# One decoder layer on one core: the second expert matmul of the late tiles as three products of rounded parts, one tile later, and the last tile added by one-hot matmuls

## The chip, the cores and the metric

The kernel runs on one core of a Trainium2 chip. The time is that of one execution on the device, in microseconds (us); the numbers shown are medians over runs of the same program on the same inputs.

## The reference

One decoder layer: self-attention, cross-attention to 1500 context rows, and a mixture of experts, each followed by a residual sum and a layer norm. The change lies in the third part, for 16 x 56 = 896 tokens of width 256, 8 experts of hidden width 1024 and two experts per token:

```python
def _L0_ffn_ref(inputs, gate_w, gate_b, w1, b1, w2, b2):
    gate_probs = softmax(x @ gate_w + gate_b, axis=-1)
    weights, selected = jax.lax.top_k(gate_probs, 2)
    weights = weights / jnp.sum(weights, axis=-1, keepdims=True)
    comb = jnp.zeros((n, E)).at[arange(n)[:, None], selected].set(weights)
    h = jax.nn.gelu(jnp.einsum('nd,edf->enf', x, w1) + b1[:, None, :])
    expert_out = jnp.einsum('enf,efd->end', h, w2) + b2[:, None, :]
    return jnp.einsum('ne,end->nd', comb, expert_out)
x = _layernorm(x + _L0_attn_ref(x, ...)); x = _layernorm(x + _L0_xattn_ref(x, ctx, ...))
x = _layernorm(x + _L0_ffn_ref(x, ...))
```

## The kernel before

The attention parts take the first 740 us of the span and are not touched. Each token's row, with its two gate values, is scattered by GpSimd into `xs` in DRAM, sorted by expert in groups of 128 rows. The residual rows (the input of the experts) go to `sums` in DRAM.

The expert stage works through `GT` = 21 tiles `g` of 128 sorted rows, each of one expert. A table `e_tab` names the expert of a tile; its first `EARLY` = 5 entries are known early, the rest after the last tokens are routed (`at["late tiles known"]`). All of `w2` (8 experts, 8 blocks of 128 x 256 each) lies in SBUF in `w2_sb`; `w1` of the tile's expert (1 MB) is loaded for each tile into one of two buffers. The steps of a tile are:

- SyncE: `load_xg(g)` loads the 128 rows when `gate(g-2)` has read the buffer (`row_read`); `load_w1(g)` loads the weights when the first matmuls of tile g-2 are done (`m1_done`). All of this stands in one queue, in order.
- TensorE: `tx(g)` transposes the rows (2 matmuls), `m1(g)` in two halves of 8 matmuls each with 128 columns makes the hidden values, `m2(g)` in 8 fp32 matmuls of 256 columns the output. `m2(g)` waits for the gelu of its tile.
- ScalarE: `gelu_half(g, i)`, four activations of 128 x 128 for each half, into `hT`.
- VectorE: `xgT_step(g)` copies the transposed rows out of PSUM, `gate(g)` makes the gate value from six small operations, `y_step(g)` scales `b2` (L918), and forms gate x output + gate x b2 (L924) in `y_sb`.
- GpSimd: `add(g)` adds the rows of `y_sb` to `sums` in DRAM by an indirect DMA (L1245); each waits until the one before has landed.

A sub-block of `w2_sb` is picked by a register that is read from `e_tab` (`value_load`), on each engine that needs the expert. TensorE's order is `tx(g)`, `m2(g-1)`, `m1(g)` for each late tile: `m2(g-1)` is the work beside which gelu and the copies run.

The end: when all 21 additions have landed (`added`), SyncE loads `sums` in four parts of two token tiles (`sum_in[q]`, L1116) into `acc`. VectorE makes statistics of each part (L967, L970, L972), GpSimd the power -1/2 (L1274), and ScalarE (parts 0 and 2) or VectorE (parts 1 and 3, `normalise`, L960) the normalised rows, which SyncE stores.

PSUM has eight banks. Banks 1 to 4 (`H_BANK` + 0 to 3) hold the hidden values of two tiles, banks 6 and 5 (`Y_BANKS`) the outputs.

For keys and values of the attention part the kernel already uses products of rounded parts: a tensor is written once in the type float32r (`ctx_hi`, `wkv_hi`), the rest beside it (`ctx_lo`, `wkv_lo`), and three products (hi hi, hi lo, lo hi, the list `SPLIT`) are summed in PSUM (`unit`, L1514 and L1521).

## Time and profile before

| | us |
|---|---|
| median of 3 runs | 913.03 (911.96 to 915.29) |
| the profiled execution, its own time | 917.23 |
| its span, first to last instruction | 915.4 |
| TensorE busy in the span | 830.5 (91%) |
| VectorE, ScalarE, GpSimd busy | 599.3, 465.5, 267.4 |

Instruction names give the output and the inputs without the digits at a name's end or before an underscore (`w2_sb` is shown as `w_sb`). One fp32 matmul stands in the trace as two records, one float32r matmul as one. A matmul's shown duration is longer than the distance to the next one, since they are pipelined; the pace is read from the start times. "PEclk" is the granted clock of TensorE: 1.00 is 2.4 GHz and 0.50 is 1.2 GHz.

### The profile page before, as it was taken

How to read it: one execution, taken by the hardware profiler on the slowest of the kernel's cores; microseconds unless marked ns; L12 is line 12 of the kernel's file. 1: busy time of each engine (PE TensorE's matmuls, PEld its weight loads, DVE VectorE, ACT ScalarE, POOL GpSimd, SP SyncE). 2: the span in 40 equal slices, each digit the busy share in tenths (PEclk: the TensorE clock that was granted, in tenths of full speed). 3: DMA queues.
4: the chain of work that ended last, by engine and by line, in shares of the span. 5: the costliest groups of instructions: out<-in, count | busy, mean ns of one | idle time of the engine just before them, and what ended most of it. 6: DMA issues, size and time to landing. Idle time of an engine off the chain costs nothing.

```text
span 915.4 us, 29917 instructions
## 1 busy us (share of the span) xinstructions
PE 830.5 (91%) x12210; PEld 669.4 (73%) x12210; DVE 599.3 (65%) x1308; ACT 465.5 (51%) x1050; POOL 267.4 (29%) x341
## 2 busy tenths in 40 slices
PE   5789999999999989999999999999997889999992
PEld 3567876777777767777777777777775589999991
DVE  5867677777787758777787777777864734222222
ACT  2355565655565546555665655556654443332232
POOL 5142224122612251244215232612240103222222
PEclk9899999999999999999999999999999699999997
DMA  6355545454454545545455455544474646766643
GB/s 214 108 168 155 155 121 159 131 148 131 141 162 133 143 130 154 149 148 162 136 144 175 131 155 143 166 125 144 142 251 163 260 170 188 182 184 190 189 124 98
DMA packets 91092, 143.56 MB, mean 157 GB/s; under 512 B 11378, under 2 KB 79794, under 8 KB 87120
## 3 DMA queue, kind: packets, MB, share of 16 engines
q1 hardware_dynamic: 86592, 132.59, 48.4%
q0 software_dynamic: 4368, 9.08, 4.4%
q8 instruction: 99, 1.62, 0.8%
q14 instruction: 33, 0.27, 0.1%
HBM read 101.60 MB, written 39.94 MB: 155 GB/s over the span
## 4 chain that ended last, share of the span: by engine, by line
PE 60%; DMA 15%; ACT 8%; DVE 7%; SPq 5%; issue 4%; POOL 0%; DVEq 0%; POOLq 0%; ACTq 0%
PE ps L1521 11%; DMA k_dram<-k_two 11%; PE ps L1514 9%; PE ps L1831 8%; PE ps L1852 8%; PE ps L1595 6%; PE ps L1573 5%; PE ps L1537 4%; SPq L1006 3%; ACT k_two L1297 3%; DMA k_st<-k_dram 3%; ACT pT L1324 2%; DVE negmax L484 2%; DVE k_two L478 2%; PE ps L1638 2%
## 5 line engine op out<-in xcount | busy, mean ns | idle before, releaser
L484 DVE TENSOR_REDUCE negmax<-ps 112x1 f32<-112x1500 f32 x121 | 207.3, 1713 | 42.0 <-PE ps L1537 41.0
L1324 ACT ACTIVATE pT<-ps 125x448 f32<-125x448 f32 x384 | 196.1, 547 | 22.4 <-PE ps L1573 18.4
L1155 POOL TENSOR_TENSOR ctx_lo<-ctx_raw,ctx_hi 128x250 fp32r<-128x250 f32 x188 | 130.5, 726 | 234.7 <-DVE ctx_hi L469 234.7
L1573 PE MATMUL ps<-qbd,k_st 98*128 98x112 f16 x1536 | 130.1, 216 | 17.2 <-ACT qbd L1280 8.1
L1573 PEld LDWEIGHTS ps<-qbd,k_st 98*128 98x128 f16 x1536 | 87.4, 99 | 76.2 <-ACT qbd L1280 23.1
L478 DVE SCALAR_TENSOR_TENSOR k_two<-ps,bk_sb,k_two 128x500 f16<-128x500 f32 x96 | 70.7, 736 | 88.3 <-ACT k_two L1297 88.2
L1297 ACT ACTIVATE k_two<-ps,bk_sb 128x500 f16<-128x500 f32 x96 | 65.0, 677 | 95.7 <-PE ps L1514 77.3
L1280 ACT COPY v_sb<-ps 125x512 f32<-125x512 f32 x96 | 56.3, 587 | 105.6 <-PE ps L1521 105.6
L1595 PE MATMUL ps<-pT,v_sb 125*17 125x56 f32 x6144 | 92.8, 217 | 8.3 <-issue 8.3
L1537 PE MATMUL ps<-k_st,qbd 96*112 96x500 f16 x363 | 96.9, 374 | 2.9 <-issue 2.4
L1595 PEld LDWEIGHTS ps<-pT,v_sb 125*17 125x17 f32 x6144 | 81.1, 100 | 24.5 <-issue 18.1
L1452 ACT ACTIVATE hT<-ps,b_col 128x128 f32<-128x128 f32 x168 | 48.0, 368 | 99.9 <-PE ps L1831 99.9
L1521 PE MATMUL ps<-wkv_hi,ctx_hi 128*125 128x256 f32 x384 | 88.2, 311 | 6.2 <-DVE k_two L478 4.1
L1831 PE MATMUL ps<-xgT,w_sb 128*128 128x128 f32 x672 | 80.6, 279 | 0.0
L1831 PEld LDWEIGHTS ps<-xgT,w_sb 128*128 128x128 f32 x672 | 79.9, 195 | 1.0
L1521 PE MATMUL ps<-wkv_hi,ctx_lo 128*125 128x256 f32 x384 | 77.7, 284 | 2.7 <-issue 2.7
L1521 PE MATMUL ps<-wkv_lo,ctx_hi 128*125 128x256 f32 x384 | 77.5, 283 | 0.0
L1852 PE MATMUL ps<-w_sb,hT 128*128 x336 | 76.2, 380 | 0.6 <-issue 0.6
L1521 PEld LDWEIGHTS ps<-wkv_hi,ctx_hi 128*125 128x125 f32 x384 | 60.7, 189 | 21.7 <-issue 18.6
L1514 PE MATMUL ps<-ctx_hi,wkv_hi 128*128 128x500 f32 x192 | 68.4, 438 | 7.6 <-ACT v_sb L1280 3.4
L1245 POOL DMA_INDIRECT sums<-y_sb,g_token x21 | 32.9, 1567 | 137.4 <-DVE y_sb L924 134.2
L1852 PEld LDWEIGHTS ps<-w_sb,hT 128*128 128x128 f32 x336 | 62.1, 190 | 8.7 <-issue 1.1
(238 smaller groups left out, 1220.5 us busy)
## 6 DMA issues: line engine op xcount, KB each, us to landing
k_st<-k_dram SPq DMA_DIRECT2D x288, 125.0 KB, 2.6
w_sb<-w SPq DMA_DIRECT2D x25, 1024.0 KB, 5.7
ctx_raw<-ctx_T SPq DMA_DIRECT2D x48, 500.0 KB, 4.3
k_dram<-k_two SPq DMA_DIRECT2D x96, 250.0 KB, 3.7
xs<-zeros SPq DMA_DIRECT2D x28, 260.0 KB
w_sb<-w POOLq DMA_DIRECT2D x4, 1024.0 KB, 9.5
xg<-xs SPq DMA_DIRECT2D x21, 130.0 KB, 4.7
a_x<-x_tok SPq DMA_DIRECT2D x8, 128.0 KB, 2.4
```

Source lines behind the costliest of these rows:

```text
L478: V.scalar_tensor_tensor(k_two[:, i, 1], ps[:, BANK_KV, 0:MC], bk_sb[:, g:g + 1], k_two[:, i, 0], ALU.add, ALU.subtract).then_inc(unit_out, 1)
L484: V.tensor_reduce(negmax[0:QW], ps[0:QW, BANK_S:BANK_S + CHUNKS, 0:MC], AX.XY, ALU.max, negate=True).then_inc(max_done, 1)
L1155: last = nc.gpsimd.tensor_tensor(ctx_lo[:, k, c2, a], ctx_raw[:, k, c2, a], ctx_hi[:, k, c2, a].bitcast(F32), ALU.subtract)
L1297: nc.scalar.activation(k_two[:, i, 0], ps[:, BANK_KV, 0:MC], ACT.Identity, bias=bk_sb[:, g:g + 1]).then_inc(k_hi_done, 1)
L1324: nc.scalar.activation(pT[0:MT, (PAIRS * b + p) % 3, TPC * g:TPC * g + TPC], ps[0:MT, BANK_T + n % 2, 0:TPC * QW].rearrange("p (t n) -> p ...
L1514: last = mm(ps[:, BANK_KV, 0:MC], ws[w][:, k, P * g:P * g + P], cs[x][:, place, k, :], start=(i == 0 and k == 0), stop=(i == 2 and k == CH ...
L1521: last = mm(ps[0:MT, BANK_KV, D * m:D * m + D], cs[x][:, place, k, a:a + MT], ws[w][:, k, D:2 * D], start=(i == 0 and k == 0), stop=(i == ...
L1537: last = mm(ps[0:QW, BANK_S + c, 0:MC], qbd[0:KS, j, p].rearrange("p h s -> p (h s)"), k_st[0:KS, j, p, MC * c:MC * c + MC], start=True, s ...
L1573: last = mm(ps[:, BANK_T + n % 2, QW * i:QW * i + QW], k_st[:, j, p, a:a + P], qbd[:, j, p].rearrange("p h s -> p (h s)"), start=True, sto ...
L1595: last = mm(ps[32 * i:32 * i + VW, BANK_O, QW * (p % 4) + S * hp:QW * (p % 4) + S * hp + S], v_sb[0:MT, j, m, 2 * p + hp], pT[0:MT, (PAIRS ...
L1831: last = mm(ps[:, H_BANK + 2 * par + i, P * q:P * q + P], w1_sb[:, par, c, P * f:P * f + P], xgT[:, par, c], start=(c == 0), stop=(c == CH ...
L1852: last = mm(ps[:, Y_BANKS[g % 2], 0:D], hT[:, g % 2, f], w2_sb[:, bass.ds(e, 1), f].rearrange("p a n -> p (a n)"), start=(f == 0), stop=(f ...
```

## The change

For tiles 5 to 20, ScalarE writes `w2_hi` (2048 columns, the tile's expert copied to float32r) and `h_hi` (1024 columns, the gelu's output copied to float32r); VectorE writes the differences `w2_lo` and `h_lo`. `m2_split(g)` makes 24 float32r matmuls of 256 columns instead of 8 fp32 matmuls, and TensorE's order becomes first half of `m1(g)`, `tx(g+1)`, second half of `m1(g)`, `m2_split(g-1)`. `w2_hi(g)` waits until `m2_split(g-2)` is done (two buffers).

The last tile is no longer added in DRAM. SyncE waits for 20 additions, TensorE brings each loaded part of the sums into PSUM by a product with the identity (`carried(q)`, fp32, 512 columns) and adds, for each of 8 token tiles, a one-hot matrix times `y_sb` (fp32, 256 columns). The one-hot matrices are made by VectorE from `token_row`. Statistics and normalisation read the sums from PSUM.

```diff
@@ -235,10 +235,16 @@
         xg = sb("xg", [P, 2, XW])
         xgT = sb("xgT", [P, 2, CH, P])
         y_sb = sb("y_sb", [P, 2, D])
-        sb("to_values", [P, 6392])
+        w2_hi = sb("w2_hi", [P, 2, FT, D], F32R)
+        h_hi = sb("h_hi", [P, 2, FT, P], F32R)
+        sb("to_values", [P, 248])
         b2_all = sb("b2_all", [P, E, D])
         hT = sb("hT", [P, 2, FT, P])
         g_b2 = sb("g_b2", [P, 4, D])
+        token_row = sb("token_row", [P, P])
+        token_hot = sb("token_hot", [P, TILES, P])
+        w2_lo = sb("w2_lo", [P, 2, FT, D], F32R)
+        h_lo = sb("h_lo", [P, 2, FT, P], F32R)
         kv_in = sem("kv_in")
         dec_in = sem("dec_in")
@@ -899,6 +917,8 @@
                 one = slice(q, q + 1)
                 if g == EARLY:
                     dve.wait_ge(p_dve, at["late tiles known"])
+                if g > EARLY:
+                    dve.wait_ge(added, 16 * (g - 3))
                 V.scalar_tensor_tensor(g_num[:, one], row[:, D + 2:D + 3], e_sum[:, g:g + 1], row[:, D + 1:D + 2],
                                        ALU.is_equal, ALU.max).then_inc(gate_step, 1)
                 V.tensor_scalar(g_den[:, one], row[:, D + 1:D + 2], 1.0, None, ALU.add).then_inc(gate_step, 1)
@@ -947,24 +967,52 @@
             gate(3)
             late_table()
             y_step(2)
-            for g in range(3, GT):
+            xgT_step(4)
+            gate(4)
+            y_step(3)
+            xgT_step(EARLY)
+            gate(EARLY)
+            y_step(EARLY - 1)
+
+            def w2_lo_step(g):
+                e = dve.value_load(e_tab[0:1, g:g + 1], min_val=0, max_val=E - 1)
+                dve.wait_ge(w2_hi_done, g - EARLY + 1)
+                V.tensor_tensor(w2_lo[:, g % 2], w2_sb[:, bass.ds(e, 1)].rearrange("p a f n -> p (a f) n"),
+                                w2_hi[:, g % 2].bitcast(F32), ALU.subtract).then_inc(w2_lo_done, 1)
+
+            def h_lo_step(g):
+                dve.wait_ge(h_hi_done, g - EARLY + 1)
+                V.tensor_tensor(h_lo[:, g % 2], hT[:, g % 2], h_hi[:, g % 2].bitcast(F32),
+                                ALU.subtract).then_inc(h_lo_done, 1)
+
+            for g in range(EARLY, GT):
                 if g + 1 < GT:
                     xgT_step(g + 1)
+                w2_lo_step(g)
+                if g + 1 < GT:
                     gate(g + 1)
-                y_step(g)
+                h_lo_step(g)
+                if g > EARLY:
+                    y_step(g - 1)
+                if g == GT - 1:
+                    dve.wait_ge(row_kept, 1)
+                    for t in range(TILES):
+                        V.tensor_scalar(token_hot[:, t], token_row[:], float(P * t + 1), xg[:, (GT - 1) % 2, D:D + 1],
+                                        ALU.add, ALU.is_equal).then_inc(hot_made, 1)
+            y_step(GT - 1)
             def normalise(q):
                 dve.wait_ge(f_rstd, q + 1)
                 for t in (2 * q, 2 * q + 1):
-                    V.tensor_scalar(o_all[:, t], acc[:, t], mv8[:, t, 0:1], sm[:, 5, t:t + 1],
+                    V.tensor_scalar(o_all[:, t], last_sum(t), mv8[:, t, 0:1], sm[:, 5, t:t + 1],
                                     ALU.subtract, ALU.mult).then_inc(f_out[q], 1)
             for q in range(TILES // 2):
                 two = slice(2 * q, 2 * q + 2)
-                dve.wait_ge(sum_in[q], 16)
+                dve.wait_ge(hot_done, 2 * q + 2)
                 for t in (2 * q, 2 * q + 1):
-                    V.bn_stats(st8[:, t], acc[:, t]).then_inc(f_stat, 1)
+                    V.bn_stats(st8[:, t], last_sum(t)).then_inc(f_stat, 1)
                 for t in (2 * q, 2 * q + 1):
                     dve.wait_ge(f_stat, 2 * q + t + 1)
                     V.bn_aggr(mv8[:, t], st8[:, t]).then_inc(f_stat, 1)
@@ -1111,7 +1159,7 @@
                 load_xg(g)
                 load_w1(g)
-            sp.wait_ge(added, 16 * GT)
+            sp.wait_ge(added, 16 * (GT - 1))
             for q in range(TILES // 2):
                 sp.dma_start(acc[:, 2 * q:2 * q + 2], sums_tiles[2 * q:2 * q + 2].rearrange("t p n -> p t n")).then_inc(sum_in[q], 16)
             out_rows = out.rearrange("(t j) p n -> j p t n", j=2)
@@ -1265,7 +1313,7 @@
             add(1)
             scatter(TILES - 1)
             pool.wait_ge(sums_last, 16)
-            for g in range(2, GT):
+            for g in range(2, GT - 1):
                 add(g)
             for q in range(TILES // 2):
@@ -1460,15 +1508,32 @@
             gelu_half(1, 0)
             gelu_half(1, 1)
             b_step(4, TILES - 1)
+            def w2_hi_step(g):
+                act.wait_ge(p_dve, at["late tiles known"])
+                e = act.value_load(e_tab[0:1, g:g + 1], min_val=0, max_val=E - 1)
+                act.wait_ge(m2_done, g - 1)
+                copy(w2_hi[:, g % 2], w2_sb[:, bass.ds(e, 1)].rearrange("p a f n -> p (a f) n")).then_inc(w2_hi_done, 1)
+
+            def h_hi_step(g):
+                act.wait_ge(gelu_done, 2 * g + 2)
+                copy(h_hi[:, g % 2], hT[:, g % 2]).then_inc(h_hi_done, 1)
+
             for g in range(2, GT):
+                if g >= EARLY:
+                    w2_hi_step(g)
+                if g == EARLY:
+                    act.wait_ge(row_made, 1)
+                    copy(token_row[:], ps[:, BANK_O, 0:P]).then_inc(row_kept, 1)
                 gelu_half(g, 0)
                 gelu_half(g, 1)
+                if g >= EARLY:
+                    h_hi_step(g)
             for q in (0, 2):
                 act.wait_ge(f_mean, q // 2 + 1)
                 act.wait_ge(f_rstd, q + 1)
                 for t in (2 * q, 2 * q + 1):
-                    nc.scalar.activation(o_all[:, t], acc[:, t], ACT.Identity, bias=sm[:, 6, t:t + 1]).then_inc(f_centre, 1)
+                    nc.scalar.activation(o_all[:, t], last_sum(t), ACT.Identity, bias=sm[:, 6, t:t + 1]).then_inc(f_centre, 1)
                 for t in (2 * q, 2 * q + 1):
                     act.wait_ge(f_centre, t + 1 - q)
                     nc.scalar.activation(o_all[:, t], o_all[:, t], ACT.Copy, scale=sm[:, 5, t:t + 1]).then_inc(f_out[q], 1)
@@ -1853,6 +1918,17 @@
                               w2_sb[:, bass.ds(e, 1), f].rearrange("p a n -> p (a n)"), start=(f == 0), stop=(f == FT - 1))
                 last.then_inc(m2_done, 1)
+            def m2_split(g):
+                par = g % 2
+                pe.wait_ge(y_ready, g - 1)
+                pe.wait_ge(w2_lo_done, g - EARLY + 1)
+                pe.wait_ge(h_lo_done, g - EARLY + 1)
+                for f in range(FT):
+                    for i, (x, w) in enumerate(SPLIT):
+                        last = mm(ps[:, Y_BANKS[par], 0:D], (h_hi, h_lo)[x][:, par, f], (w2_hi, w2_lo)[w][:, par, f],
+                                  start=(f == 0 and i == 0), stop=(f == FT - 1 and i == 2))
+                last.then_inc(m2_done, 1)
+
             last_tile = TILES - 1
             pe.wait_ge(p_dve, at["early tiles known"])
             tx(0)
@@ -1882,11 +1958,32 @@
             m2(3)
             m1(4)
             pe.wait_ge(p_dve, at["late tiles known"])
+            tx(EARLY)
+            m2(EARLY - 1)
+            pe.wait_ge(y_ready, EARLY - 1)
+            mm(ps[:, BANK_O, 0:P], ones16[:], before16[:], start=True, stop=True).then_inc(row_made, 1)
             for g in range(EARLY, GT):
-                tx(g)
-                m2(g - 1)
-                m1(g)
-            m2(GT - 1)
+                m1_half(g, 0)
+                if g + 1 < GT:
+                    tx(g + 1)
+                m1_half(g, 1)
+                if g > EARLY:
+                    m2_split(g - 1)
+            m2_split(GT - 1)
+
+            def carried(q):
+                pe.wait_ge(sum_in[q], 16)
+                mm(ps[:, H_BANK + q].rearrange("p (t n) -> p t n", t=2), id32[:], acc[:, 2 * q:2 * q + 2],
+                   start=True, stop=False)
+
+            carried(0)
+            carried(1)
+            pe.wait_ge(y_ready, GT)
+            for t in range(TILES):
+                if t % 2 == 0 and t > 2:
+                    carried(t // 2)
+                pe.wait_ge(hot_made, t + 1)
+                mm(last_sum(t), token_hot[:, t], y_sb[:, (GT - 1) % 2], start=False, stop=(t % 2 == 1)).then_inc(hot_done, 1)
 # ---- launch: one core; the arrays only change their layout ----
```

TensorE's queue at a late tile, before (two matmul rows of the eight; "ISA" sets the address from the register). This is the place after `m1(4)`:

```order
L1831 MATMUL ps<-xgT,w_sb 128x128 x16
L1482 MATMUL ps<-id,xg 128x128 x2
L1810 TENSOR_LOAD e_tab
L1810 ISA x2
L1852 ISA
L1852 MATMUL ps<-w_sb,hT 128x256
L1852 ISA
L1852 MATMUL ps<-w_sb,hT 128x256
```

The same queue of the changed kernel, from the end of `m2(4)` on (L1896 is `m1_half`, L1547 the transposes, L1928 `m2_split`, of whose 24 rows three stand here):

```order
L1964 MATMUL ps<-before,ones 128x128
L1896 MATMUL ps<-xgT,w_sb 128x128 x8
L1547 MATMUL ps<-id,xg 128x128 x2
L1896 MATMUL ps<-xgT,w_sb 128x128 x16
L1547 MATMUL ps<-id,xg 128x128 x2
L1896 MATMUL ps<-xgT,w_sb 128x128 x8
L1928 MATMUL ps<-w_hi,h_hi 128x256
L1928 MATMUL ps<-w_lo,h_hi 128x256
L1928 MATMUL ps<-w_hi,h_lo 128x256
```

The second matmuls of tile 5 now stand behind the first ones of tile 6; before they stood ahead of them.

VectorE's queue of the changed kernel through one late tile (L912 `xgT_step`, L978 and L980 `w2_lo_step`, L922 to L930 `gate`, L985 `h_lo_step`, L934 to L944 `y_step` of the tile before):

```order
L912 COPY xgT<-ps 128x256 [waits tx_done]
L978 TENSOR_LOAD e_tab
L978 ISA x2
L980 ISA [waits w2_hi_done]
L980 TENSOR_TENSOR w_lo<-w_sb,w_hi 128x2048
L922 SCALAR_TENSOR_TENSOR g_num<-xg,e_sum 128x1 [waits added]
...
L930 TENSOR_TENSOR g_gate<-g_num,g_rec 128x1 [waits gate_step]
L985 TENSOR_TENSOR h_lo<-hT,h_hi 128x1024 [waits h_hi_done]
L934 TENSOR_LOAD e_tab
...
L938 TENSOR_SCALAR g_b<-b_all,g_gate 128x256
L944 SCALAR_TENSOR_TENSOR y_sb<-ps,g_gate,g_b 128x256 [waits added,m2_done,gate_done]
```

Before, the queue held `xgT_step`, `gate` and `y_step` alone; `w2_lo` and `h_lo` and a second register load have come in.

TensorE's last rows of the changed kernel (L1976 is `carried`, L1986 the one-hot products), which have no counterpart before:

```order
L1976 MATMUL ps<-rows_all,id 128x512 x2
L1986 MATMUL ps<-y_sb,token_hot 128x256 x4
L1976 MATMUL ps<-rows_all,id 128x512
L1986 MATMUL ps<-y_sb,token_hot 128x256 x2
L1976 MATMUL ps<-rows_all,id 128x512
L1986 MATMUL ps<-y_sb,token_hot 128x256 x2
```

Two identity products stand ahead of the first one-hot products, so the statistics of part 0 come after four products.

## Rows read from the trace of the kernel before

**Rows 1.** The page: busy time, and the granted clock in 40 slices

```profile
PE 830.5 (91%) x12210; PEld 669.4 (73%) x12210; DVE 599.3 (65%) x1308; ACT 465.5 (51%) x1050; POOL 267.4 (29%) x341
PEclk9899999999999999999999999999999699999997
```

**Rows 2.** The chain that ended last, 700 to 916 us: start, us, what

```profile
886.71 0.22 PE ps L1482 x2
886.92 3.46 PE ps L1852 x16
890.38 3.57 PE ps L1831 x32
893.95 3.52 PE ps L1852 x16
...
897.55 0.49 DVE y_sb L924
...
898.79 3.72 DMA sums<-y_sb,g_token
```

**Rows 3.** Stretches: us; busy PE, PEld, DVE, ACT, POOL; PEclk; DMA share; GB/s

```profile
780.00:890.00 110.00, 110.00 (x757) 103.49 (x756) 29.82 (x136) 34.31 (x120) 23.39 (x15) 1.00 0.65 178
```

**Rows 4.** Timeline of TensorE, 300 to 312 us: start, us, what

```profile
304.66 0.40 PE L1521 MATMUL ps<-wkv_lo,ctx_hi 128*125 128x256 f32 x2
...
305.60 0.40 PE L1521 MATMUL ps<-wkv_hi,ctx_lo 128*125 128x256 f32 x2
```

**Rows 5.** Lines L439 and L1280: duration ns min/median/max, first and last start

```profile
L439 DVE TENSOR_TENSOR wkv_lo<-pT,wkv_hi x1: 1224/1224/1224, 6.1 to 6.1; 128x1024 fp32r<-128x1024 f32 x1
...
L1280 ACT COPY v_sb<-ps x96: 586/587/592, 15.1 to 698.1; 125x512 f32<-125x512 f32 x96
L1280 ACT COPY a_oT<-ps x8: 372/372/373, 33.9 to 627.0; 128x256 f32<-128x256 f32 x8
L1280 ACT COPY rows_all<-b_x x8: 407/431/433, 193.0 to 758.7; 128x256 f32<-128x256 f32 x8
```

**Rows 6.** Timeline of one late tile, 845 to 870 us

```profile
850.61 1.14 ACT L1452 ACTIVATE hT<-ps,b_col 128x128 f32<-128x128 f32 x4 [0.66 <-PE ps L1831]
850.66 0.42 DVE L894 COPY xgT<-ps 128x256 f32<-128x256 f32 x1 [3.25 <-PE ps L1482]
851.00 0.21 DVE L902 SCALAR_TENSOR_TENSOR g_num<-xg,e_sum 128x1 f32<-128x1 f32 x1
...
851.70 0.16 DVE L910 TENSOR_TENSOR g_gate<-g_num,g_rec 128x1 f32<-128x1 f32 x1
```

**Rows 7.** Timeline of the end, 890 to 916 us

```profile
890.47 0.48 DVE L924 SCALAR_TENSOR_TENSOR y_sb<-ps,g_gate,g_b 128x256 f32<-128x256 f32 x1 [1.36 <-PE ps L1852]
891.25 0.35 DVE L918 TENSOR_SCALAR g_b<-b_all,g_gate 128x256 f32 x1 [0.29 <-issue]
...
902.52 1.95 SPq L1116 DMA_DIRECT2D rows_all<-sums  x4
905.25 0.75 DVE L967 BATCH_NORM_STATS2 st<-rows_all 128x6 f32<-128x256 f32 x2 [7.21 <-DMA rows_all<-sums]
...
909.41 0.75 DVE L967 BATCH_NORM_STATS2 st<-rows_all 128x6 f32<-128x256 f32 x2
```

**Rows 8.** Stretches of the end and of two earlier places, columns as in Rows 3

```profile
897.50:898.50 1.00, 0.00 (x0) 0.00 (x0) 0.48 (x1) 0.00 (x0) 0.00 (x0) 1.00 0.00 0
...
901.50:902.00 0.50, 0.00 (x0) 0.00 (x0) 0.00 (x0) 0.00 (x0) 0.00 (x0) 0.81 0.87 131
902.00:904.00 2.00, 0.00 (x0) 0.00 (x0) 0.00 (x0) 0.00 (x0) 0.00 (x0) 0.50 0.13 36
...
22.00:27.80 5.80, 5.80 (x18) 2.96 (x19) 5.33 (x11) 0.63 (x1) 0.34 (x1) 0.50 0.52 122
...
741.50:744.70 3.20, 3.20 (x17) 3.20 (x16) 1.10 (x3) 0.00 (x0) 0.00 (x0) 0.50 0.00 0
```

**Rows 9.** DMA queue, issues from 770 to 900 us: KB each, median us to landing

```profile
w_sb<-w SPq DMA_DIRECT2D x16, 1024.0 KB, 5.7
```

More of the change, by code:

```diff
@@ L346, in decoder_layer @@
         sums_last = sem("sums_last")
+        row_made = sem("row_made")
+        w2_hi_done = sem("w2_hi_done")
+        w2_lo_done = sem("w2_lo_done")
+        h_hi_done = sem("h_hi_done")
+        h_lo_done = sem("h_lo_done")
+        row_kept = sem("row_kept")
+        hot_made = sem("hot_made")
+        hot_done = sem("hot_done")
         tail_set = sem("tail_set")
@@ L398, in home, with last_sum @@
             return BANK_S if t == 0 and k in (2, 4, 6) else BANK_A
+        def last_sum(t):
+            return ps[:, H_BANK + t // 2, D * (t % 2):D * (t % 2) + D]
         def key_place(par, c, g):
```

## The prediction

> **What bounds the kernel now.** I read the page first: TensorE is busy for 91% of the span, and its granted clock is at the full level in nearly every slice but the last [rows 1]. The attention part is untouched, so only the stretch after 778 us matters. There the stretch view says it plainly: from 780 to 890 us TensorE is busy for 110.00 of 110.00 us at clock 1.00, VectorE for 29.82 and ScalarE for 34.31 [rows 3]. The chain that ended last holds nothing but TensorE in that stretch, one tile after the other: transposes 0.22, second matmuls 3.46, first matmuls 3.57, so 7.25 us a tile [rows 2]. TensorE's time per tile is what a change can win. After the last tile the bound changes: output scaled (897.55 to 898.04), addition landed at 902.51, loads of the sums issued from 902.52, first statistics at 905.25, statistics of part 3 at 909.41, end of the span at 915.4 [rows 2, 7]. I call the end of the last tile's first matmuls T, before 893.95: the tail behind T is 21.45 us long.
>
> **The tiles: TensorE.** The second matmuls of tiles 5 to 20 become 24 float32r products of 256 columns. The kernel has this form already, in the value units of the attention part: with weights of 125 columns instead of 128, two matmuls start at 304.66 and the fifth pair at 305.60, so four pairs take 0.94 us and one matmul 0.1175 us [rows 4]. An fp32 one takes 3.46 / 8 = 0.4325 us [rows 2], so three products are 0.35 against 0.43, and a tile's 24 are 2.82 us against 3.46. Bounds: 2.82 if the pace holds, 3.46 if the change of form gains nothing; I take 2.82, since shape and form are the same but for three columns. Before T, fifteen second matmuls of late tiles stood (5 to 19); now fourteen do (5 to 18), since they come one tile later. So T comes 15 x 3.46 - 14 x 2.82 = 51.9 - 39.5 = **12.4 us earlier**, if nobody makes TensorE wait. The one bf16 product for `token_row` and its copy are below 0.5 us and are left out. A tile now takes 0.22 + 3.57 + 2.82 = 6.61 us.
>
> **The tiles: the engines beside it.** ScalarE gets a copy of 2048 and one of 1024 columns. Copies of 512 and 256 columns take 0.587 and 0.372 us [rows 5], 0.84 ns a column, which gives 1.88 and 1.02 us; in proportion to the larger copy, the upper bound, it is 2.35 and 1.17. With the two gelu halves of 1.14 each [rows 6] that is 5.2 to 5.8 us a tile, under 6.61. `w2_hi(g)` may start when `m2_split(g-2)` ends, which is just the start of `m1(g)`; it ends some 1.9 us later, about when the first half of `m1(g)` (1.79 us) is done, so gelu is hardly late.
>
> VectorE is the tighter one. Per tile: copy 0.42 [rows 6]; register load, of which 0.36 shows (from the start of the operation ahead to the one behind the load 0.78 us pass in the row pair 890.47 and 891.25 [rows 7], less 0.42 of work); `w2_lo` at most twice the 1.224 us that the same subtraction takes at 1024 columns, 2.45 [rows 5]; gate 851.00 to 851.86, 0.86 [rows 6]; `h_lo` 1.22; `y_step` 0.35 + 0.48 [rows 7]; four waits at some 0.05. Sum 6.34 against 6.61. Cover: counted from the start of `m1(g)`, `h_lo(g)` ends at about 7.5 us, and `m2_split(g)` wants it at 6.61 + 3.79 = 10.4, so 2.9 us are in hand. If VectorE needs x us a tile, TensorE loses 14 (x - 6.61) - 2.9 us in all: nothing up to x = 6.8.
>
> Weights: `w1(g+2)` is asked for when `m1(g)` ends, at 3.8 us after its start, and lands 5.7 later [rows 9], at 9.5 to 10; it is wanted at 13.2. The rows of `xg` are asked for after each `gate` and have two tiles. `add(g)` takes 4.5 us from y to landing [rows 2], against 6.61 a tile, so the new wait in `gate` (addition g-3) is long over. All this costs nothing as long as it lies beside 6.61 us of TensorE.
>
> **The tail.** From the new T: the second half of gelu ends at T + 1.35, `h_hi` at + 2.4, `h_lo` at + 3.65, `y_step(19)` (it stands behind `h_lo(20)`) at + 4.6. `m2_split(19)` ended at + 2.8, so TensorE waits 0.9 us, then makes `m2_split(20)` until + 6.5; `y_sb` of tile 20 is ready near + 7.5, with the eight one-hot matrices made beside it. Addition 19 lands 4.5 after + 4.6, the first sums 2.7 after that: **T + 11.8**. Before, the first sums were there at T + 11.3: the spared addition is paid back by the last output's place one tile further back.
>
> Then comes what is new: TensorE must make 4 identity products of 512 columns (2 x 0.4325 = 0.865 each) and 8 one-hot products (0.4325 each), 6.92 us at full clock [rows 2]. The clock is not full there. TensorE stopped at 897.5, and the granted clock fell to 0.50 near 901.8, 4.3 us later [rows 8]; now it stands still from + 6.5 to + 11.8. How soon it returns: in two stretches in which TensorE was busy without a pause, it was at 0.50 for 3.2 us (from 741.5) and for 5.8 us (from 22.0) [rows 8]. I take 5 us. In these 5 us half the work is done, 2.5, and the rest takes 4.4: the last one-hot product is done 9.4 us after the first sums. Statistics of part 3 cannot start before `normalise(1)` is over, at about + 9.9, and from them to the end it is 6.0 us as before (909.41 to 915.4) [rows 7]. End: T + 11.8 + 9.9 + 6.0 = T + 27.7, against T + 21.45. The tail costs **6.2 us more**.
>
> By the Trainium skill (TensorE: Matmul & The Clock Gate, "What's actually happening") the array sits at 1.2 GHz by default and goes back to it when idle; the clock column of this trace agrees, with 0.50 after the stop.
>
> **Sum.** -12.4 + 6.2 = -6.2 us. The profiled execution has a span of 915.4 in a time of 917.23, 4.2 above the median; the differences are taken to be the same for both. 913.03 - 6.2 = 906.8, so **907**.
>
> **Rivals.**
> - **The clock stays low through all twelve products** (a 0.50 stretch of 5.8 us is in the trace, and the twelve have pauses only if sums land late). 13.8 us instead of 9.4 and no wait for `normalise`: + 4.0, 910.8. Chance 0.1.
> - **The clock does not fall, or comes back at once.** The products take 6.9 us, and part 3 starts at + 7.2: - 2.7, 904.2. For it: the pause is only 5.3 us, little over the 4.3 after which it fell. Chance 0.15.
> - **Addition 19 is held up by the one-hot matrices.** They stand directly behind `y_step(19)` on VectorE, when GpSimd prepares this addition, which everything behind waits for. Eight operations of about 0.2 us (the 256-column one is 0.35 [rows 7]) are 1.6 us: 908.4. In the trace of before no VectorE work lies beside an addition's preparation at the end, so it shows neither. Chance 0.08. The Trainium skill (SBUF — State Buffer, "SBUF: two separate sides") says that GpSimd cannot write its descriptors while VectorE runs an operation in a two-port mode; no row here shows it.
> - **VectorE becomes the bound (slower).** By the formula above the gain is gone at x = 7.26 us a tile and the time is 0.5% above before (917.6) at x = 7.6, that is 1.2 us over my sum; for instance if the register loads or the 2048 columns cost half as much again. Against it: every part but `w2_lo`'s length has a row. 913 to 918, chance 0.07.
> - **The float32r products don't keep their pace.** At 0.144 us each a tile's second matmuls stay at 3.46; only the shift by one tile is left: - 3.5 + 6.2, 915.7. For it: in the units the weights have 125 columns, here 128. Chance 0.05.
> - Something unpriced (rows or weights late, a wait at the first split tile): 909 to 914, chance 0.05.
>
> My forecast itself has 0.5 and its own range is 905 to 909.
>
> **How the numbers follow.** A measurement of this kernel tells about 0.5% (4.6 us) from no change, so faster is below 908.5. From the forecast's 0.5 some 0.43 lie below, from the high-clock case all 0.15, from the held addition 0.04: 0.62. Slower (above 917.6) is what is left of the VectorE and pace cases with some for the unknown, 0.08. Same 0.30. The range reaches down to the high-clock case and up past the low-clock one: 903.5 to 912.5.
>
> **What the profile after would show.** Right: 6.6 us between `m2_split` groups with TensorE busy throughout, 24 matmuls at 0.118 us; VectorE at 5.5 to 6.4 us a tile with its wait on transposes still there; T near 881.5; first sums near T + 11.8; clock at 0.50 when the first identity product starts. Wrong: TensorE waiting for `h_lo` in every tile (VectorE), 3.4 us for a tile's 24 products (pace), clock 1.00 in the tail, or an addition landing later than 4.5 us after y.

## Result

The changed kernel takes 905.09 us (median of 20 runs, 900.23 to 914.34), the kernel before 914.44 us (20 runs, 906.66 to 925.74). The ratio, taken over the executions outside the slower state that a few of them fell in, is 0.9925, 95% interval 0.9901 to 0.9948: 6.9 us less, between 4.8 and 9.1. The two medians are 9.4 us apart, just outside that interval; single executions of one kernel scatter by 14 to 19 us, so I go by the ratio. Forecast was 6.2 us less.

The profiled execution of the changed kernel has a span of 905.0 us, against 915.4 before. Of these 10.4 us only a part belongs to the change: the first matmuls of tile 0 start at 736.91 instead of 741.51, after a part of the program in which no instruction differs. Over the 14 profiles of this study that start lies between 729.4 and 743.6 us with no relation to the edit, while the stage behind it was 128.1 and 127.7 us in two traces of the changed kernel. Of the kernel before there is one trace, but from M to T, defined below, the run with the one-hot end alone, which has the same instructions there, agrees with it within 0.1 us (112.4 and 112.3). So I compare kernels by the stage from the end of tile 4's second matmuls (M) to the end of the span: 133.8 us before (781.63 to 915.4), 128.1 after (776.90 to 905.0). **The change is worth 5.7 us in the traces.**

The chain of the changed kernel, start, us, what. The first rows are tiles 4, 5 and 18 (L1917 second matmuls in fp32, L1928 the split ones, L1896 the first ones), the others the end:

```profile
773.44 3.46 PE ps L1917 x16
...
784.63 3.07 PE ps L1928 x24
787.70 1.78 PE ps L1896 x16
789.48 0.22 PE ps L1547 x2
789.70 1.79 PE ps L1896 x16
791.49 2.83 PE ps L1928 x24
...
870.93 2.83 PE ps L1928 x24
873.76 3.58 PE ps L1896 x32
...
882.58 3.92 DMA sums<-y_sb,g_token
...
886.51 2.73 DMA rows_all<-sums
...
889.29 3.78 PE ps L1976 x4
893.07 2.25 PE ps L1986 x8
```

The second matmuls take 2.83 us instead of 3.46 [rows 2], the tile 6.62 instead of 7.25. The first matmuls of tile 20 end at T = 877.34, so M to T is 100.4 us; before it was 112.3. The tail behind T is 27.7 us long instead of 21.45.

The stretches, columns as in Rows 3: TensorE has no pause up to T, VectorE is busy for 82 of 100 us, and the clock falls in the pause before the sums land and comes back at 894.

```profile
776.90:877.30 100.40, 100.36 (x881) 100.20 (x881) 81.86 (x165) 78.95 (x155) 31.82 (x15) 1.00 0.64 190
...
886.00:887.00 1.00, 0.00 (x0) 0.00 (x0) 0.00 (x0) 0.00 (x0) 0.00 (x0) 1.00 0.03 3
887.00:888.00 1.00, 0.00 (x0) 0.00 (x0) 0.00 (x0) 0.00 (x0) 0.00 (x0) 0.58 0.20 59
...
893.00:894.00 1.00, 1.00 (x4) 0.82 (x3) 0.00 (x0) 0.00 (x0) 0.00 (x0) 0.50 0.00 0
894.00:897.00 3.00, 3.00 (x13) 2.26 (x13) 2.27 (x11) 0.41 (x2) 0.81 (x2) 1.00 0.00 0
```

One thing got worse that the span does not show. GpSimd's additions by their source line, first of the kernel before, then of the changed one. The first row has shortest, median and longest preparation in ns and the time of the first and the last; the second row the time to landing, which is counted from the start of the preparation and so contains it:

```profile
L1245 POOL DMA_INDIRECT sums<-y_sb,g_token x21: 1549/1561/1612, 752.6 to 898.8; - x21
...
DMA to landing us min/median/max: 3.6/3.8/4.2
```

```profile
L1293 POOL DMA_INDIRECT sums<-y_sb,g_token x20: 1549/2087/3229, 748.0 to 882.6; - x20
...
DMA to landing us min/median/max: 3.7/5.2/7.1
```

Preparing one takes 2.09 us in the median instead of 1.56, and preparation and landing together 5.2 instead of 3.8. From tile 6 to tile 19 every addition starts 0.78 us after the landing of the one ahead; before the change none of the late ones did, there were 3.3 us or more between them. The additions of tiles 6 to 19 start at 798.85 to 882.58, one in 6.44 us, where a tile takes 6.62: the delay that tiles 5 and 6 leave (7.1 us each to landing) is only just made up at the end. Addition 19 starts 0.78 us after its output and 0.78 us after the landing of addition 18 (both at 881.80), so two paths set the start of the sums at once. Several of the experiments below ran into this.

### The profile page after: what moved, and what is told of

Its sections match the earlier page's. It is cut to its first block, busy times and chain, and to the rows that moved or that the text cites. A ratio compares the mean times of both kernels' runs of the same rounds, so it can differ in the third digit from the quotient of the medians.

```text
span 905.0 us, 30247 instructions
## 1 busy us (share of the span) xinstructions
PE 828.6 (92%) x12363; PEld 671.4 (74%) x12363; DVE 656.6 (73%) x1348; ACT 511.9 (57%) x1083; POOL 276.5 (31%) x340
## 3 DMA queue, kind: packets, MB, share of 16 engines
q8 instruction: 99, 1.62, 0.8%
## 4 chain that ended last, share of the span: by engine, by line
PE 61%; DMA 13%; DVE 9%; ACT 8%; SPq 4%; issue 4%; DVEq 0%; POOL 0%; POOLq 0%; ACTq 0%
PE ps L1586 11%; PE ps L1579 10%; DMA k_dram<-k_two 9%; PE ps L1896 9%; PE ps L1660 7%; PE ps L1638 5%; PE ps L1928 4%; PE ps L1602 4%; ACT k_two L1345 3%; SPq L1054 3%; DMA k_st<-k_dram 3%; ACT pT L1372 2%; DVE negmax L502 2%; PE ps L1917 2%; DVE k_two L496 2%
## 5 line engine op out<-in xcount | busy, mean ns | idle before, releaser
L1203 POOL TENSOR_TENSOR ctx_lo<-ctx_raw,ctx_hi 128x250 fp32r<-128x250 f32 x188 | 130.5, 726 | 230.9 <-DVE ctx_hi L487 230.9
L1896 PE MATMUL ps<-xgT,w_sb 128*128 128x128 f32 x672 | 83.0, 279 | 0.0
L1896 PEld LDWEIGHTS ps<-xgT,w_sb 128*128 128x128 f32 x672 | 79.8, 195 | 0.3
L1293 POOL DMA_INDIRECT sums<-y_sb,g_token x20 | 42.2, 2111 | 118.1 <-DVE y_sb L944 62.0
L1232 POOL TENSOR_TENSOR qbd<-q_st,pmask 96x448 f16<-96x448 f16 x32 | 29.2, 932 | 129.4 <-DVE q_st L604 129.4
L1328 ACT COPY qbd<-ps 2x112 f16<-2x112 f16 x128 | 31.4, 245 | 61.0 <-PE ps L1624 58.9
```

The source lines that it names most:

```text
L1203: last = nc.gpsimd.tensor_tensor(ctx_lo[:, k, c2, a], ctx_raw[:, k, c2, a], ctx_hi[:, k, c2, a].bitcast(F32), ALU.subtract)
L1328: return nc.scalar.copy(dst, src)
L1896: last = mm(ps[:, H_BANK + 2 * par + i, P * q:P * q + P], w1_sb[:, par, c, P * f:P * f + P], xgT[:, par, c], start=(c == 0), stop=(c == CH ...
```

## Experiments

All stages, from M to the end of the span; T is the end of tile 20's first matmuls. Runs without a ratio were run once. Each ratio is to the kernel before as run in the same set; the sets were run on different chips.

| run | M | span | stage | ratio to before |
|---|---|---|---|---|
| before | 781.63 | 915.4 | 133.8 | 1 |
| the change | 776.90 | 905.0 | 128.1 | 0.9925 (0.9901 to 0.9948) |
| the change again | 783.51 | 911.2 | 127.7 | 0.9947 (0.9907 to 0.9987) |
| split products alone | 781.06 | 907.6 | 126.5 | 0.9933 (0.9891 to 0.9976) |
| one-hot end alone | 778.10 | 908.6 | 130.5 | 0.9952 (0.9921 to 0.9982) |
| tile 19 early | 779.04 | 907.5 | 128.5 | 0.9914 (0.9879 to 0.9949) |
| TensorE kept busy in the pause | 774.09 | 899.8 | 125.7 | 0.9926 (0.9888 to 0.9963) |
| two products of three | 772.48 | 887.5 | 115.0 | |
| 128 columns of w2_lo | 769.37 | 897.5 | 128.1 | |
| tile 19 early, tile 20 in fp32 | 774.39 | 901.4 | 127.0 | 0.9920 (0.9878 to 0.9961) |
| the same, TensorE kept busy | 776.11 | 900.5 | 124.4 | 0.9916 (0.9886 to 0.9945) |
| w2_lo twice | 778.12 | 923.1 | 145.0 | |
| tile 19 early, little w2_lo and w1 | 779.12 | 905.1 | 126.0 | |
| split alone, little w2_lo and w1 | 775.51 | 902.3 | 126.8 | |

The intervals of the ratios are 4 to 8 us wide and overlap throughout; differences of 1 to 4 us between these kernels are shown by the stages, one trace each, and not by the clocked runs.

**The change again.** The same file.

> The changed kernel as it is, beside the three others on one chip. All theories: 0.9925 of before (0.990 to 0.995), stage after the second matmuls of tile 4 near 128.1 us; the part ahead of that stage should differ from before by chance alone.

Stage 127.7 against 128.1 us: two traces of one kernel lie 0.4 us apart. The start of the stage moved by 6.7 us between them. The clocked ratio is 0.9947 and its interval holds the first one's 0.9925.

The chain that ended last takes another way here. It runs through all 15 additions from tile 5 on without a break, 797.58 to 892.98, three quarters of the stage; its last rows are:

```profile
883.34 5.20 DMA sums<-y_sb,g_token
...
889.32 3.65 DMA sums<-y_sb,g_token
...
892.99 2.71 DMA rows_all<-sums
```

Addition 18 landed at 888.54, 0.13 us after output 19 was there (888.41). So in the changed kernel the row of additions is as much the bound of the last sums as TensorE is, and in the first trace the two only met.

**Each half of the change alone.** First the split products with the end as before:

```diff
-            sp.wait_ge(added, 16 * (GT - 1))
+            sp.wait_ge(added, 16 * GT)
-            for g in range(2, GT - 1):
+            for g in range(2, GT):
                 add(g)
-                dve.wait_ge(hot_done, 2 * q + 2)
+                dve.wait_ge(sum_in[q], 16)
```

(and `last_sum(t)` is `acc[:, t]`; `token_row`, `token_hot`, `carried` and the one-hot products are gone.)

> The products of rounded parts as in the change, the last tile added in DRAM as before. Theory (what the one-hot end is worth here is negative): with the split order the sums can be loaded only 11.9 us after the last first matmuls (T) and 12 products follow at half clock; without them, tile 20's output is ready at T + 7.2, lands at T + 11.7, the first sums are there at T + 14.4, and from there 10.15 us as before: T + 24.6 instead of the changed kernel's T + 27.7. So 3.1 us less than the changed kernel, stage after the second matmuls of tile 4: 125.0 us instead of 128.1. Rival (the one-hot end saves the 4.5 us of an addition): 3 us or more above the changed kernel, stage 131 or more.

126.5 us: better than the change by 1.5 (by 1.2 than its repeat), not by 3.1. Its chain shows why:

```profile
880.81 5.10 DMA sums<-y_sb,g_token
...
886.68 3.54 DMA sums<-y_sb,g_token
...
891.00 3.77 DMA sums<-y_sb,g_token
...
894.79 2.84 DMA rows_all<-sums
```

Addition 20 starts at 891.00, after the landing of addition 19 at 890.22, while its output was ready at 888.84. I had let it start from its own output. The one-hot end costs 1.2 to 1.5 us in this order of work, by one trace of each, where its rival had it gain 3.

Then the one-hot end alone, on the kernel before (fp32 second matmuls and their order kept):

```diff
-            for g in range(2, GT):
+            for g in range(2, GT - 1):
                 add(g)
+            carried(0)
+            carried(1)
+            pe.wait_ge(y_ready, GT)
+            for t in range(TILES):
+                ...
+                mm(last_sum(t), token_hot[:, t], y_sb[:, (GT - 1) % 2], ...)
```

(`token_row`, `token_hot`, `last_sum` and the waits are as in the change.)

> The one-hot end alone, second matmuls in fp32 and in the order of before. Theory (the end is good where the last output but one is early and TensorE has no pause): addition 19 lands at T + 1.5, first sums at T + 4.2, TensorE comes from the last second matmuls at T + 3.5 without a fall of the clock, 6.9 us of products at full clock, end at T + 17.5 instead of T + 21.5: 4.0 us less than before, 909 to 911 where before is 914. Rival (the one-hot end costs its products whatever the order): at least 3 us more than before.

130.5 us, 3.2 less than before; expected 4.0. Here addition 19 runs beside the first matmuls of tile 20, and the first identity products need 0.99 us for each of the two at full clock:

```profile
888.29 3.88 DMA sums<-y_sb,g_token
...
892.19 2.99 DMA rows_all<-sums
...
895.22 1.98 PE ps L1914 x4
897.21 1.73 PE ps L1924 x8
```

So the halves are worth 7.2 and 3.2 us alone, 10.4 in sum, and 5.7 together. The traces say where the missing 4.7 us are. M to T is the same with and without the one-hot end (100.4 and 100.3 us split, 112.4 and 112.3 in fp32). From T to the first sums the one-hot end alone has 4.65 us and the change 11.9, 7.25 more; without the one-hot end it is 11.3 before and 16.25 with split products, 5.0 more. That is 2.3 us: output 19, for which the sums wait with the one-hot end, comes 4.5 us after T and not 3.0 before it, while output 20, which counts without it, moves by less. From the first sums to the end of the span the one-hot end alone takes 13.5 us, at clock 1.00 all through its products, and the change 15.7, with a pause of TensorE and a fallen clock; without the one-hot end this part is 10.2 and 10.0. That is the other 2.4, and the next run takes it away.

**The clock in the pause.**

```diff
             m2_split(GT - 1)
+            for _ in range(11):
+                mm(ps[:, BANK_S, 0:D], id32[:], w2_sb[:, 0, 0], start=True, stop=True)
```

> The changed kernel with 11 more fp32 matmuls of 256 columns on TensorE in the pause between the last split tile and the first sums; their result is not used. Theory (the clock's fall in that pause has a price): granted clock 1.00 when the first identity product starts, the twelve products take 6.9 instead of 9.4 us, of which the statistics' own pace leaves 1.5 to 2.5 us: 1.5 to 2.5 us less than the changed kernel. Rival (loads and statistics set the pace of the end): less than 0.5 us.

The granted clock is 1.00 from 880 to 892 us, and the first two identity products take 1.99 us instead of 3.78:

```profile
883.60 2.79 DMA rows_all<-sums
...
886.43 1.99 PE ps L1978 x4
888.41 1.73 PE ps L1988 x8
```

Stage 125.7 us, 2.4 less (2.0 less than the repeat). The sums land 112.3 us after M in both kernels, so all of it is behind that landing, where only the clock of the products differs. That the pause costs a clock level and that the level has this price is shown.

**Where VectorE stands.** Two products of the three:

```diff
-                    for i, (x, w) in enumerate(SPLIT):
+                    for i, (x, w) in enumerate(SPLIT[:2]):
```

> The third product (lo of the hidden values times hi of the weights) is left out in tiles 5 to 20; VectorE and ScalarE do all they did, so the output loses some precision. TensorE then needs 0.22 + 3.57 + 1.88 = 5.67 us a tile. Theory (VectorE is next, at about 6.1 to 6.2 us a tile): the tile period falls from 6.62 to 6.1 to 6.2, not to 5.67, and TensorE waits for h_lo or the transposed rows in every tile. Rival (there is room on VectorE): 5.67 to 5.8 us a tile, 14 us less in all.

The stage is 115.0 us, 13.1 less. M to T is 87.0 us instead of 100.4, 13.4 less, which is 14 x 0.96: the tile takes 5.66 us and VectorE keeps up. My theory of it as the next bound at 6.1 is refuted. Behind T nothing is won, though two more tiles are shorter there: addition 19 starts 1.55 us after its output, held by the row of additions, and the sums land 12.9 us after T instead of 11.9. VectorE's timeline through one such tile, one `y_step` (L944) to the next:

```profile
835.36 0.48 DVE L944 SCALAR_TENSOR_TENSOR y_sb<-ps,g_gate,g_b 128x256 f32<-128x256 f32 x1
835.76 0.41 DVE L912 COPY xgT<-ps 128x256 f32<-128x256 f32 x1
836.12 2.29 DVE L980 TENSOR_TENSOR w_lo<-w_sb,w_hi 128x2048 fp32r<-128x2048 f32 x1
...
839.49 1.23 DVE L985 TENSOR_TENSOR h_lo<-hT,h_hi 128x1024 fp32r<-128x1024 f32 x1 [0.31 <-ACT h_hi L1328]
840.63 0.35 DVE L938 TENSOR_SCALAR g_b<-b_all,g_gate 128x256 f32 x1
841.02 0.48 DVE L944 SCALAR_TENSOR_TENSOR y_sb<-ps,g_gate,g_b 128x256 f32<-128x256 f32 x1
```

An operation starts some 0.06 to 0.09 us before the shown end of the one ahead (835.36 + 0.48 is 835.84, the next starts at 835.76), and the register load that I had put at 0.36 us is hidden: `w2_lo` starts at 836.12, before the copy's end. In the changed kernel, where VectorE first waits 0.40 us for the transposes, the load still shows as 0.33 us without work between the copy and `w2_lo`; it vanishes when VectorE has work queued.

Then `w2_lo` twice in each tile:

```diff
                 dve.wait_ge(w2_hi_done, g - EARLY + 1)
+                V.tensor_tensor(w2_lo[:, g % 2], w2_sb[...], w2_hi[:, g % 2].bitcast(F32), ALU.subtract).then_inc(twice, 1)
+                dve.wait_ge(twice, g - EARLY + 1)
                 V.tensor_tensor(w2_lo[:, g % 2], ...
```

> The changed kernel with w2_lo computed twice in each tile, 2.3 us more of VectorE. With two products only, VectorE kept up with 5.67 us a tile, so its own need is 5.3 to 5.6 us and now 7.6 to 7.9. Theory (the formula of the prediction: nothing until the need is over 6.6 us a tile, then 14 times the excess less 2.9 us in hand): 11 to 15 us more than the changed kernel, stage 139 to 143. Rival (the 2.9 us in hand aren't there, or more waits come in): over 146.

```profile
793.11 1.22 DVE L989 TENSOR_TENSOR h_lo<-hT,h_hi 128x1024 fp32r<-128x1024 f32 x1
...
840.91 2.29 DVE L981 TENSOR_TENSOR w_lo<-w_sb,w_hi 128x2048 fp32r<-128x2048 f32 x1
843.24 2.29 DVE L984 TENSOR_TENSOR w_lo<-w_sb,w_hi 128x2048 fp32r<-128x2048 f32 x1
...
891.72 1.22 DVE L989 TENSOR_TENSOR h_lo<-hT,h_hi 128x1024 fp32r<-128x1024 f32 x1
```

Thirteen tiles in 98.61 us are 7.585 us each. The extra operation and its wait are 2.33, and VectorE's operations follow each other there with no gap of 0.05 us or more, so its own need in the changed kernel is 5.26 us a tile, against my 6.34. The stage is 145.0 us, 16.9 more: above the 139 to 143 of the theory and below the rival's 146. 14 x (7.585 - 6.61) is 13.7, and T comes 13.6 us later against M (114.0 instead of 100.4), so the 2.9 us in hand were not there. The rest (3.3) is behind T, where the doubled `w2_lo` also stands ahead of the last `h_lo`; how it divides I did not separate.

**The output of tile 19 early.**

```diff
+                if g == GT - 1:
+                    m2_split(g - 1)
                 m1_half(g, 1)
-                if g > EARLY:
+                if EARLY < g < GT - 1:
                     m2_split(g - 1)
```

(and on VectorE `y_step(GT - 2)` ahead of `h_lo_step(GT - 1)`.)

> The changed kernel with the second matmuls of tile 19 between the two halves of tile 20's first ones, and its output scaled ahead of h_lo(20). Theory (the end hangs on the output of tile 19): with s the start of tile 20's first matmuls, output 19 is ready at s + 5.1 instead of s + 8.1, first sums at s + 12.5, TensorE busy to s + 12.9 with a short pause, 12 products at full or nearly full clock: 4 to 5 us less than the changed kernel. Rival (the end hangs on TensorE's clock or on tile 20's chain through gelu, h_hi and h_lo, which gets 2.8 us later): no gain or up to 2 us more.

128.5 us: no gain, though output 19 was ready at 881.14, 2.8 us earlier against M than in the change (102.1 instead of 104.9). The chain does not hold TensorE here but additions:

```profile
872.81 5.28 DMA sums<-y_sb,g_token
...
878.87 5.24 DMA sums<-y_sb,g_token
...
884.88 4.75 DMA sums<-y_sb,g_token
...
889.65 2.73 DMA rows_all<-sums
```

Addition 19 starts at 884.88, 3.75 us after its output, because addition 18 landed at 884.10, and the first sums are there 113.3 us after M, 1.0 later than in the change. The rival had the result (no gain), but neither theory had named this cause. Two runs ask what slows the additions. First little of `w2_lo` (from tile 7 on only 128 of its 2048 columns are written, and VectorE waits there for the second matmuls of tile g-2):

> From tile 7 on VectorE writes only 128 of the 2048 columns of w2_lo, the rest keeps what tiles 5 and 6 left, so the output is not exact. TensorE does the same work. Theory (additions are slowed because GpSimd prepares them while VectorE subtracts with two inputs from SBUF): the preparations beside tiles 8 to 19 fall from 2.1 us in the median to 1.56, the landing from 5.2 to 3.8 us as before, and no addition waits for the one ahead. Rival (the denser weight loads slow them): landing stays at 5 us. Neither changes the time of the kernel by more than 1 us.

```profile
L1298 POOL DMA_INDIRECT sums<-y_sb,g_token x20: 1549/1560/1655, 740.5 to 875.0; - x20
...
DMA to landing us min/median/max: 3.7/5.8/6.8
```

The preparation falls back to 1.56 us, as the theory says: it is `w2_lo` beside it that makes it long. Preparation and landing together do not get shorter: 5.8 us, as the rival says, though 0.5 us of preparation are spared. So two things slow an addition, and they don't add up: what is spared in the preparation is spent waiting behind it. The second was tried on the kernel with tile 19 early, with little `w2_lo` and, from tile 7 on, 128 of 1024 columns of the `w1` load:

```diff
-                sp.dma_start(w1_sb[:, g % 2], w1[bass.ds(e, 1)]...)
+                n = F if g < EARLY + 2 else P
+                sp.dma_start(w1_sb[:, g % 2, :, 0:n], w1[bass.ds(e, 1), :, :, 0:n]...)
```

> Tile 19 early, and from tile 7 on only 128 of 2048 columns of w2_lo and 128 of 1024 columns of the first weights (w1) loaded, so the output is not exact; TensorE's work is the same. Theory (the chain of additions is the bound of that run: they are slowed by w2_lo in their preparation and by the w1 loads in their landing, so that addition 19 starts 3 us late): preparation 1.56 and landing 3.7 to 4.0 us, addition 19 starts 0.7 us after its output, the products start when TensorE comes from tile 20: stage 124.5 to 125.5 instead of 128.5. Rival (something else holds the end): 127.5 or more, and if landing stays over 5 us the w1 loads are not what slows it.

```profile
L1301 POOL DMA_INDIRECT sums<-y_sb,g_token x20: 1549/1561/1627, 750.2 to 882.9; - x20
...
DMA to landing us min/median/max: 3.7/3.9/4.2
```

Landing is 3.9 us, where little `w2_lo` alone left it at 5.8: it is the `w1` transfer beside it, 1 MB in each tile, which in the changed kernel is under way when the addition's rows move, and before the change had mostly landed by then. With little `w2_lo` alone, for instance, the load asked for at 843.70 landed 5.2 us later, at 848.9, and the addition begun at 844.02 landed at 849.9, just behind it. It is a matter of when and not of how much: with `w2_lo` twice the loads are full too, but their rows have moved before the addition's, and from the end of its preparation an addition takes 2.2 us to land as before the change (5.5 less 3.24). What a small `w1` load does with a full `w2_lo` was not run.

The stage is 126.0 us, 2.5 less than with full loads and 0.5 to 1.5 more than expected. Addition 19 starts 1.7 us after its output and not 0.7: outputs 18 and 19 are 3.55 us apart here, and even an unslowed addition with the 0.78 us to the next takes 4.5. The chain now goes through tile 20 instead: TensorE waits for its gelu, `h_hi` and `h_lo`, the clock falls in that pause, and the 24 products take 5.46 us instead of 2.83:

```profile
884.83 1.24 DVE h_lo L990
...
886.20 5.46 PE ps L1936 x24
```

The same reliefs on the split products alone:

> The products of rounded parts without the one-hot end, with the same two reliefs as in the run with tile 19 early (128 columns of w2_lo and of w1 from tile 7 on; output not exact). Theory: addition 20 starts 0.7 us after its output instead of after the landing of addition 19: 1.4 us less than with full loads, stage 125.1 instead of 126.5. Rival: unchanged at 126.5.

126.8 us, no gain, a miss: even at 3.75 us an addition, 20 waits for 19 (they start at 881.05 and 885.58 in its chain), since outputs 19 and 20 are 3.0 us apart. What holds that kernel is that two additions must follow each other behind output 19, and not how slow the ones ahead of them are.

**Tile 20 in fp32.** The kernel with tile 19 early, and the last second matmuls as before:

```diff
-            m2_split(GT - 1)
+            m2(GT - 1)
```

(and no `w2_hi`, `w2_lo`, `h_hi`, `h_lo` for that tile.)

> The run with tile 19 early, and tile 20's second matmuls in fp32 as before, without its hi and lo parts. Theory: the chain gelu, h_hi, h_lo behind tile 20 (3.7 us, in which TensorE stands) is spared for 0.63 us more of matmuls; the twelve products start when the sums land, 1 to 3 us earlier than with tile 19 early alone, at full clock: 5 to 7 us less than the changed kernel. Rival (the sums' landing is the bound whatever TensorE does): the same as with tile 19 early within 0.5 us.

127.0 us, 1.5 less than with tile 19 early alone and 1.1 less than the change, not 5 to 7. The sums land at 884.94, 110.6 us after M, 1.8 earlier than in the change; but TensorE had stopped at 881.1 and its clock falls at 884.3, shortly before:

```profile
882.11 2.83 DMA rows_all<-sums
...
884.98 3.78 PE ps L1982 x4
888.76 2.96 PE ps L1992 x8
```

So the same with 9 unused matmuls in the pause:

> Tile 19 early, tile 20's second matmuls in fp32, and 9 unused fp32 matmuls of 256 columns in the pause before the sums land. In the run without them the stage after tile 4's second matmuls is 127.0 us, the sums are there 110.6 us after these, and the clock falls 0.6 us before they land, so that the first five products run at 0.50. Theory (addition chain sets the start, clock the rest): clock 1.00, 6.9 us of products, stage 124.0 us, 1.7 less than the warm run alone and 10 less than before. Rival (the start of the sums is what counts): 126.5 to 127.

124.4 us, as the theory had it (124.0), 3.7 less than the change and 9.4 less than before. Clocked it is 0.9916 (0.9886 to 0.9945), which can't be told from the change's 0.9925. It is the shortest stage among the kernels here that do all the work.

## Why the prediction was right

- **Pace of the products.** Predicted 2.82 us a tile, measured 2.83. The float32r form of the attention part gave the price, and weights of 128 columns instead of 125 cost nothing that can be seen.
- **T earlier by 12.4 us.** Measured 11.9 (112.3 to 100.4). The 0.5 us are, as far as the chain shows, the extra small product, a first split tile of 3.07 us, and roundings.
- **The engines beside it.** They cost nothing, as predicted, with more room than I gave them. `w2_lo` took 2.29 us, not 2.45; by the Trainium skill (VectorE: DVE Perf Modes, "The perf-mode tier table (the rule you actually need)") an fp32 `tensor_tensor` of 2048 elements takes 2293 ns, and the trace agrees. ScalarE's copies took 1.90 and 1.05 us against 1.88 and 1.02. VectorE's total was the mis-sized one: 5.26 us against 6.34, since I added shown durations, which overlap, and counted a register load that is hidden when VectorE has no pause. The load was misread too: the row at 890.47 has 0.48 us of work and not 0.42, so 0.30 of the 0.78 us show [rows 7]. The 2.9 us in hand were not there either when VectorE was made the bound. Neither mattered at 6.62 us a tile.
- **First sums at T + 11.8.** Measured 889.24 - 877.34 = 11.9. That it fits this closely is partly luck: I had derived it from output 19 alone, and the row of additions, which I had taken to cost nothing, reached the same moment within 0.1 us in the first trace and 0.13 us later in the repeat.
- **The twelve products at falling and rising clock.** Predicted 9.4 us with 5 at half clock. They ran from 889.29 to 898.8, with 0.50 until 894.0, 4.7 us. The statistics of part 3 start at T + 21.7 predicted, 899.14 or T + 21.8 measured. The price of the clock, 2.7 in the rival, was 2.4 (2.0 against the repeat) when its fall was taken away.
- **The tail costs 6.2 us.** Measured 27.7 - 21.45 = 6.2.
- **The step that failed without harm:** "`add(g)` takes 4.5 us from y to landing against 6.61 a tile, so the new wait is long over". An addition took 5.2 us in the median from the start of its preparation to landing (3.8 before), started up to 4.1 us after its output because it queued behind the one ahead, and one came in 6.44 us; there was almost no room left. The prediction had named an addition landing later than 4.5 us after y as a sign of being wrong; from tile 5 on every one did. The new wait itself, in `gate`, still cost nothing in the changed kernel, but with little `w2_lo` VectorE stood in it in ten tiles (4.5 us in all). The price of the queue is in the experiments: it took the gain of an early tile 19, and 1 us behind T with two products. The rival about addition 19 being held by the one-hot matrices did not come: its preparation took 1.62 us and started 0.78 us after the output. But what it rests on did occur in every tile ahead, beside `w2_lo`. By the Trainium skill (SBUF — State Buffer, "SBUF: two separate sides") the port pair is locked also by a VectorE operation with two SBUF inputs, against a GpSimd operation that reads SBUF; the preparations of up to 3.23 us beside `w2_lo`, and 1.56 without it, agree with a lock, though no run here tells it from another reason for which the two could get in each other's way.
- The forecast was 907 us, measured 905.09. Sum of the steps by the traces: -11.9 + 6.2 = -5.7, clocked -6.9 (4.8 to 9.1), forecast -6.2. The 907 was counted from 913.03, where the larger set of runs has 914.44.

## What to carry to other kernels

A pipeline that is made one stage deeper pays at its end: look at which output the last chain hangs on, and try the last iteration in the old, shallower order or form (here that and a TensorE kept busy gave 3.7 us together; the earlier output alone gave nothing). Work on an engine that looks idle can still queue: count the time from one issue to the next against the period, not the busy time. Two halves of a change that are good alone can hang on the same stretch at the end (here the wait for the sums), so price them together. And where a long identical part ahead varies more from run to run than the change is worth, compare the stage from a fixed point in the traces.

## What the runs showed of the hardware

- The granted clock fell from 1.00 to 0.50 in the pauses of TensorE: stop at 897.5, fall near 901.8 before the change; stop at 884.2, fall near 887.2 after it; stop at 881.1, fall near 884.3 with tile 20 in fp32; stop at 896.2, fall near 898.4 with `w2_lo` twice; stop at 882.7, fall near 887.6 on the split products alone with little `w2_lo` and `w1`; so between 2.2 and 4.9 us in these five. It came back 4.7 us into the unbroken products after the change (889.29 to 894.0), 6.1 with tile 20 in fp32 (884.98 to 891.1) and 3.1 with tile 19 early (886.12 to 889.2). Unused matmuls in the pause kept it at 1.00 and were worth 2.4 and 2.6 us.
- An indirect DMA from GpSimd was slowed in two places: its preparation took 1.56 us alone and up to 3.2 us while VectorE subtracted two tensors in SBUF, and from the end of the preparation to landing it took 2.2 us alone and 4.2 to 4.5 us while a 1 MB load was under way (5.8 to 6.0 in all, with little `w2_lo`, tiles 6 to 14).
- VectorE's shown durations overlap the next operation's by some 0.05 to 0.09 us where nothing is waited for (835.36 + 0.48 against 835.76), and ScalarE's did by 0.05 between the copy `w2_hi` and gelu (834.16 + 1.90 against 836.01 in the changed kernel), so that a sum of them over a tile overstates the engine's need.
